# Chunk attention with keys over four heads and norming on GpSimd; modulated attention's shift turned in front of the scores

## The reference, cut to what matters

```python
mod = jax.nn.sigmoid(hidden_states @ cg_W + cg_b + (cons_vec @ am_W + am_b))
scores = scores * mod.transpose(0, 2, 1)[..., None]
probs = jax.nn.softmax(scores, axis=-1)
ctx = jnp.einsum('bhqk,bhkd->bhqd', probs, v)
```

## Time and profile before

| | |
|---|---|
| median of 3 runs | 3992.09 us (3989.94 to 3993.36) |
| profiled execution | 3997.91 us, span 3996.2 us |
| PE, PEld busy | 3580.1 us (90%), 1710.4 us (43%) |
| DVE, ACT, POOL busy | 2339.2 us (59%), 1502.5 us (38%), 1540.2 us (39%) |
| modulated attention | about 212 to 957 us |
| chunk attention | about 2757 to 3020 us |

### The profile page before, as it was taken

The page is one execution under the profiler, slowest core; times in us unless marked ns, Lnnn a source line. Parts: engine busy times, 40 slices in busy tenths (PEclk is TensorE's granted clock), DMA queues, the critical chain, the costliest instruction groups (busy, mean ns, idle before and its releaser), DMA issues. The chain is left out here.

```text
span 3996.2 us, 55438 instructions
## 1 busy us (share of the span) xinstructions
PE 3580.1 (90%) x19176; PEld 1710.4 (43%) x19176; DVE 2339.2 (59%) x3916; ACT 1502.5 (38%) x2216; POOL 1540.2 (39%) x1343
## 2 busy tenths in 40 slices
PE   9989999997999889998789656687998989999995
PEld 4412222222333343333545355443554655655653
DVE  5679999994666326664632458977896631111112
ACT  2237777775444323444222334212553211111112
POOL 0142222222788505887346323144552322222221
PEclk9979999998999999999889766899999989999998
DMA  5622222221112151120622421454442123333333
GB/s 182 209 77 68 76 62 62 69 71 48 36 47 63 58 195 58 43 81 16 187 71 85 150 70 45 164 127 109 131 136 83 34 69 91 103 101 105 100 90 95
DMA packets 309775, 366.44 MB, mean 92 GB/s; under 512 B 54130, under 2 KB 241796, under 8 KB 308548
## 3 DMA queue, kind: packets, MB, share of 16 engines
q1 hardware_dynamic: 269972, 305.81, 24.4%
q0 software_dynamic: 30384, 50.90, 5.5%
q10 hardware_dynamic: 9216, 7.09, 0.6%
HBM read 228.00 MB, written 127.27 MB: 89 GB/s over the span
## 5 line engine op out<-in xcount | busy, mean ns | idle before, releaser
L626 DVE TENSOR_REDUCE modulated_mx<-modulated_ring 128x1 f32<-128x512 f32 x1024 | 651.8, 683 | 43.1 <-PE modulated_ring L533 37.4
L610 ACT ACTIVATE modulated_probs<-modulated_scores 128x1024 f32<-128x1024 f32 x512 | 496.1, 1021 | 189.1 <-PE modulated_scores L554 189.0
L3234 DVE TENSOR_TENSOR expert_h<-expert_gelu,expert_bank 128x512 f32<-128x512 f32 x128 | 88.0, 688 | 390.9 <-PE expert_bank L3163 385.4
L3205 ACT ACTIVATE expert_gelu<-expert_bank 128x512 f32<-128x512 f32 x128 | 76.4, 597 | 549.4 <-PE expert_bank L3163 546.5
L3123 POOL DMA_INDIRECT scratch_acc<-expert_y,expert_idx x64 | 100.8, 1575 | 427.5 <-DVE expert_y L3239 404.2
L1019 POOL TENSOR_TENSOR causal_total<-causal_total,causal_probs 128x1024 f32<-128x1024 f32 x96 | 227.1, 2366 | 59.1 <-ACT causal_probs L928 51.7
L1019 POOL TENSOR_TENSOR meta_total<-meta_total,meta_probs 128x1024 f32<-128x1024 f32 x96 | 227.1, 2366 | 58.7 <-ACT meta_probs L928 51.3
L950 DVE TENSOR_REDUCE meta_mx<-meta_maxima 128x2 f32<-128x1024 f32 x120 | 146.9, 1224 | 117.7 <-PE meta_maxima L815 117.1
L950 DVE TENSOR_REDUCE causal_mx<-causal_maxima 128x2 f32<-128x1024 f32 x120 | 146.9, 1224 | 117.7 <-PE causal_maxima L815 117.1
L928 ACT ACTIVATE meta_probs<-meta_scores 128x1024 f32<-128x1024 f32 x128 | 131.0, 1024 | 142.2 <-PE meta_scores L841 139.3
L928 ACT ACTIVATE causal_probs<-causal_scores 128x1024 f32<-128x1024 f32 x128 | 131.0, 1024 | 142.1 <-PE causal_scores L841 139.1
(11 more groups left out here) (546 smaller groups left out, 7521.2 us busy)
## 6 DMA issues: line engine op xcount, KB each, us to landing
scratch_v<-proj_v SPq DMA_DIRECT2D x8, 1024.0 KB, 6.8
ahead_ctx<-scratch_ctx SPq DMA_DIRECT2D x16, 512.0 KB, 4.7
scratch_M<-steps_snap SPq DMA_DIRECT2D x16, 512.0 KB, 3.3
chunk_raw_v<-scratch_v SPq DMA_DIRECT2D x64, 128.0 KB, 2.8
chunk_mem<-scratch_M SPq DMA_DIRECT2D x32, 256.0 KB, 3.0
first_wg<-x_WgT SPq DMA_DIRECT2D x8, 1024.0 KB, 5.0
first_wu<-x_WuT SPq DMA_DIRECT2D x8, 1024.0 KB, 7.1
first_wd<-x_WdT SPq DMA_DIRECT2D x8, 1024.0 KB, 6.8
```

The source lines that it names most:

```text
L610: nc.scalar.activation(probs[u % NPROBS][i][:], sc[i][:], ACT.Exp, scale=SCALE).then_inc(s_exp, 1)
L626: V.tensor_reduce(mx[h % 2][:, x // 2, 1 - j % 2, j // 2, x % 2:x % 2 + 1], ring[bank_of["max", 4 * m + j]][:], AX.X, ALU.max).then_inc(s_ ...
```

## The change

Modulated attention: PE turns the shift in front of the unit's score products and not behind; ACT copies it in front of the unit's exponentials; and DVE makes it not in one piece behind the last reduction of a half, but in three pieces behind the first, second and fourth reduction of the next unit.

Chunk attention:
- A key is written for four heads and not eight: `own` (128x4) is 1 where a feature belongs to the head with this number among its four. GpSimd needs two multiplications of 512 columns for a tile, not four. The scores take eight products of 64 rows by 64 outputs and 256 columns; the 64 rows of a product hold four heads, and the two halves of the rows write different banks. The heads lie in another order in the scores, and line 2617 of the new code reads them so.
- The norming of the probabilities (`pnorm`) goes from DVE to GpSimd, behind the expansion of the keys of the next tile.
- ACT's exponential of t stands in front of the copy of t-1. PE turns t-1 at the end of slot t, behind the context of t-2.
- In the context, the four memory products stand together and the sixteen value products behind them; the start flag is set on the first alone.
- DVE makes `own` at the stage's start from `blocks`, and GpSimd waits for it.

```diff
--- modulated attention, PE
-                for i in range(2):
-                    scores(u, i)
                 if u in turns:
                     turn_shift(turns[u])
+                for i in range(2):
+                    scores(u, i)
--- modulated attention, ACT
+                if u in turns:
+                    copy_shift(turns[u])
                 for i in range(2):
...
-                if u in turns:
-                    copy_shift(turns[u])
--- modulated attention, DVE
-                    reduce(m)
-                    if m % KT == KT - 1:
-                        make_shift(m // KT)
+                    before = m // KT - 1
+                    made_here = m % KT == 0 and before > 0
+                    reduce(m, range(0, 1))
+                    if made_here:
+                        lowest(before)
+                    reduce(m, range(1, 2))
+                    if made_here:
+                        shift_high(before)
+                    reduce(m, range(2, Q))
+                    if made_here:
+                        shift_rest(before)
--- chunk attention, GpSimd
-                        for c in range(2):
-                            for h in range(HH):
-                                ins = G.tensor_tensor(kexp[j % 2][:, c, h], kT[j][:, h, c * C64:(c + 1) * C64].unsqueeze(1).broadcast_to([P, HP, C64]),
-                                                      blocks[:].unsqueeze(2).broadcast_to([P, HP, C64]), ALU.mult)
+                        for h in range(HH):
+                            ins = G.tensor_tensor(kexp[j % 2][:, h], kT[j][:, h, :].rearrange("p (c k) -> p c k", c=2).unsqueeze(2).broadcast_to([P, 2, QUAD, C64]),
+                                                  own[:].unsqueeze(1).unsqueeze(3).broadcast_to([P, 2, QUAD, C64]), ALU.mult)
                         pool_k.done(ins)
+                    if live(at, j, 1):
+                        o = (j - 1) % 2
+                        dve_rec.wait(pool, t - 1)
+                        pe_turn.wait(pool, t - 3)
+                        pool_normed.done(G.tensor_tensor(normed[o][:], probs[o][:], rec[o][:].unsqueeze(2).broadcast_to([P, H16, C64]), ALU.mult))
--- chunk attention, PE
                         for h in range(HH):
                             for c in range(2):
-                                last = nc.tensor.matmul(sc[c * C64:(c + 1) * C64, h * HP:(h + 1) * HP, :].rearrange("p h k -> p (h k)"),
-                                                        qT[j][:, h, c * C64:(c + 1) * C64], kexp[j % 2][:, c, h].rearrange("p h k -> p (h k)"),
-                                                        start=False, stop=True, skip_group_check=True)
+                                for r in range(ROWS):
+                                    at_rows = slice(r * C64, (r + 1) * C64)
+                                    last = nc.tensor.matmul(sc[c * C64:(c + 1) * C64, r * HP + h * QUAD:r * HP + (h + 1) * QUAD, :].rearrange("p a k -> p (a k)"),
+                                                            qT[j][at_rows, h, c * C64:(c + 1) * C64], kexp[j % 2][at_rows, h, c].rearrange("p a k -> p (a k)"),
+                                                            start=False, stop=True, skip_group_check=True)
...
+                        both = [(c, h, slice(c * C64, (c + 1) * C64)) for c in range(2) for h in range(HH)]
+                        for c, h, toks in both:
+                            nc.tensor.matmul(ctxps[:, h, toks], mem[m][:, c, h * P:(h + 1) * P], qT[m][:, h, toks],
+                                             start=(c + h == 0), stop=False, skip_group_check=True)
+                        for c, h, toks in both:
+                            for r in range(PAIRS // HH):
+                                last = nc.tensor.matmul(ctxps[32 * r:32 * r + 32, h, toks], val[m][:, c, h * (PAIRS // HH) + r, :],
+                                                        probsT[m % 2][:, r // 2 * QUAD + h * 2 + r % 2, toks], start=False, stop=True, skip_group_check=True)
--- chunk attention, DVE
+            V.tensor_reduce(own[:], blocks[:].rearrange("p (a b) -> p b a", b=QUAD), AX.X, ALU.add).then_inc(s_own, 1)
...
+                        pool_normed.wait(dve, t - 3)
                         dve_rec.done(V.reciprocal(rec[o][:], sums[o][:]))
-                        dve_rec.wait(dve, t - 1)
-                        pe_turn.wait(dve, t - 3)
-                        dve_normed.done(V.tensor_tensor(normed[o][:], probs[o][:], heads(rec[o]), ALU.mult))
```

More of the change, by code:

```diff
@@ L2604, in body @@
                         pe_new.done(last)
+                    if live(at, j, 1):
+                        pool_normed.wait(pe, t - 1)
+                        act_probsT.wait(pe, t - 2)
+                        for r in range(PAIRS):
+                            last = nc.tensor.transpose(turned[:, r, :], normed[(j - 1) % 2][:, 2 * r:2 * r + 2, :].rearrange("p a k -> p (a k)"), ident[:])
+                        pe_turn.done(last)
             iterations(pe, body)
```

67 lines of the change are left out of this document (32 added, 35 removed).

## The result

The changed kernel took 3922.6 us (median of 4 runs, 3920.5 to 3923.7) against 3991.0 us (4 runs, 3983.4 to 3993.4): a ratio of 0.9829 with a 95% interval of 0.9817 to 0.9841, or 63 to 73 us less. The forecast was 3947 us in 3930 to 3972. The direction and the mechanism (rival A) came; 45 us were forecast and 68 came, so the time lies 7 us outside the range. The profiled execution took 3921.6 us (span 3919.9).

The account below looks back on a forecast made before the run. PE, busy 90% of 3996.2 us, was priced inside two stages, with a GpSimd loop setting the new chunk iteration. Modulated 18 plus chunk 27 gave 45 us: 3953 profiled, 3947 us as median, range 3930 to 3972.

Parts of the forecast that it names:

- rival A: Whole kernel: both parts gain as summed, 18 + 27 = 45 us, time 3928 to 3966 us; chance 0.66.
- Modulated, DVE's part: Modulated attention: shift operations spread between reductions cost 0.15 us a half of today's 0.41 (bounds 0 and 0.41).
- Modulated, PE and ACT: Modulated attention: turn and copy in front cost 0.5 us a half where 0.84 stood (bounds 0.22 and 1.1).
- The new wait for the bank: Modulated attention: PE, turning before the scores, waits for DVE to free a ring bank, 0.2 to 0.3 us.
- Rival B: Modulated attention gives nothing, the new bank wait taking the place of the copy's; 3965 us, chance 0.12.
- Chunk, PE: Chunk attention: scores 1.05 us (gain 0.8), context 0.45 us off, so PE's slot falls from 6.86 to 5.6 us.
- Chunk, the loop: Chunk attention: dependences through GpSimd over two tiles, 11.5 + 14.1 = 25.6 us; 25.5 taken against 28.88, gaining 27 us.
- the two events of the slow clock: Chunk attention: two stretches at 1.2 GHz behind longer PE idle lengthen the average iteration; left as they are, no gain.
- today's meeting of expansion and multiplication: Chunk attention: GpSimd's expansion and DVE's multiplication exclude each other, expansion 2.03 us instead of 1.04; change removes this.
- C: Chunk attention: GpSimd's operations meet DVE's and hold the loop, iteration 28.5 us; 3971 us, chance 0.14.
- D: Chunk attention: gaps in each slot leave PE at 1.2 GHz for much of the stage, slower, 4024 us; chance 0.08.

Follow-up runs that it names:

- Experiment 8: Changed kernel with the shift turned behind the scores and copied behind the exponentials, as before, still made in three pieces: 3939.2 us, ratio 0.9869.
- experiment 1: Kernel before with the modulated part of the change alone: 3966.6 us, ratio 0.9941.
- Experiment 9: Changed kernel with GpSimd's norming of tile t-2, not t-1, behind the expansion of tile t: 3913.7 us, ratio 0.9810.
- experiment 2: Kernel before with the chunk part of the change alone: 3945.6 us, ratio 0.9890.
- experiment 7: Changed kernel with the shift made in one piece behind a half's last reduction, turn and copy still in front: 3942.9 us, ratio 0.9876.
- experiment 3: Changed kernel with the norming of the probabilities back on DVE: 3956.7 us, ratio 0.9918.
- experiment 6: Changed kernel with the old order: probabilities turned before the context product and copied before the next exponential: 3964.2 us, ratio 0.9928.
- experiment 12: Kernel before with keys over four heads alone (two expansions, eight score products), norming on DVE: 3991.2 us, ratio 0.9997.
- experiment 4: Changed kernel with keys over eight heads again (four expansions, four score products a tile), norming on GpSimd: 3977.3 us, ratio 0.9969.
- experiment 11: Changed kernel with keys a tile ahead (GpSimd norms t-2) and small transposes behind the turning of the probabilities: 3917.8 us, ratio 0.9820.

## Why the prediction was right in kind and short in size

**Modulated, DVE's part.** 0.15 us a half for three operations between reductions; measured 0. Experiment 8 has the pieces alone at 0.41 us a half, all of it.

**Modulated, PE and ACT.** The new wait for the bank was forecast at 0.2 to 0.3 us and is 0.19; turn and wait leave 0.47, the copy 0.01, against 0.5 together. A half costs 0.48 us over eight regular units (20.88) in place of 0.65, so it saves 0.77 in place of 0.60. Over 31 halves that is 24 us, and experiment 1 measured 23.3, for a forecast of 18. Rival B (the new wait takes the place of the copy's) is refuted.

**Chunk, PE.** Scores: 1.03 us, forecast 1.05, so quarters of the array run beside each other. Context: 0.83 saved, forecast 0.45, mis-sized. Slot 5.19 us for 5.6. Neither sets the iteration.

**Chunk, the loop.** Two pairs of tiles, one with the norm, take 11.0 + 13.3 = 24.3 us against 11.5 + 14.1 = 25.6. Term by term: norming 1.90 for 2.2; reciprocal and hand-overs 0.78 for 1 (the loop's 11.0 less 10.22 of the other operations); the norm adds 2.3 for 2.6; the rest within 0.1. Against the 25.5 taken, the 1.2 us are about 10 us over eight iterations. Experiment 9 shows that the loop is the bound, by opening it, and also that it bound by 1.1 us only: in the pair with the norm the last wait is DVE's own queue, which the forecast had as a plain sum of 23.2 and which experiment 9 reached with 23.15. Two sums of the forecast are off by themselves and change little: its terms of the first loop add to 11.6, not 11.5, and PE's idle of an iteration is 25.5 - 4 x 5.6 = 3.1 us, not 2.5.

**The step that failed: "so I leave the two events of the slow clock as they are".** The seven measured iterations are 210.1 us before and 169.9 after. Of these 40.2 us, 7 x (28.88 - 24.26) = 32.3 are the regular iteration, and 5.6 + 4.0 = 9.6 the two long ones of before; the rest, -1.7, is in the short and first ones of both. Each of the two events cost 1.0 us by the longer wait and 4.6 and 3.0 us by the clock behind it. The prediction had the cause in hand, where it says that the change "removes today's meeting of expansion and multiplication", and gave this no term in the sum. That meeting is what made PE wait 2.21 us and not 1.21 in front of both events, and with the norming on GpSimd it is gone; no run removes the meeting by itself. By experiment 1, where both meetings recur and only one slow stretch, 6.6 us of the 9.6 come with the kernel and 3.0 are of one execution. Whether the clock falls behind such a wait, no run lets one foretell.

The slow clock itself is not gone. In the stretch 2802.30 to 2812.00 of after it is 0.82, about 3.5 us at 1.2 GHz, where before has about 10 (0.57 over 12.00 us) and about 7 (0.66 over 10.00). That iteration is 24.71 us, 0.45 over the regular one. The traces of experiments 8, 2 and 7, with the same chunk stage, have one such short stretch each (granted clock 0.93 over the third iteration, as over this one of after) and iterations of 24.60, 25.09 and 26.06 us: 0.34, 0.83 and 1.80 over. So a slow stretch can nearly vanish behind the loop, as PE's 5.19 us of work in 6.06 a tile would let it, but in one of four traces it was paid at about the price of before, 0.5 us for each us at 1.2 GHz. Most of what was saved comes from the waits that are gone and from the shorter stretch, not from PE's slack.

**The other miss, of size only,** is the loop's: norming, hand-overs and norm as above, about 10 us, no less than the events.

Added up: 45 us forecast; about 10 for the loop, 5 to 7 for modulated attention (23.3 to 24.8 by experiment 1's median and trace, for 18) and 6 to 10 for the events make 66 to 72, and 68 was measured.

**The rivals.** C (GpSimd meets DVE and holds an iteration at 28.5) is refuted by mean durations of 1.04 and 1.90 us and by iterations of 24.3 us. D did not happen, though it was near: the granted clock falls to 0.88 or 0.89 over iterations of experiments 3, 6 and 12, each of which lacks a part of the change or more.

**What was wrong in the reasoning behind the parts.** I priced each part by itself and added. The experiments give 34 us for the transfer, 55 for the keys, 42 for the order and 8 for the context: 139 us for a stage that gains 44. And the keys alone gain 0. Each part relieves one engine or the loop. Without the transfer, the keys or the order the iteration stays at 28 to 30 us (experiments 3, 4 and 6); only the context's grouping is a small term, 25.0 us without it.

## What to carry to other kernels

Find the loop of dependences through all engines, not only the busiest engine, and sum it operation by operation; a part that shortens one engine pays only once every other engine and the loop are below the new length. When a slow-clock event or another loss is seen in the profile of before, ask what sets it off and whether the change removes that: here a meeting of two engines did, and its removal was worth 6 to 10 us that no sum held. Treat a wait of PE of 1.5 us or more, inside a busy loop of this kind, as a risk and not as a fixed cost: the same wait was followed by 1.2 GHz in one iteration and not in the next.

## What was not expected of the hardware

- Quarters of the array work beside each other in f32: eight products of 64 rows by 64 outputs and 256 columns take 1.03 us, four of 128 rows by 64 and 512 columns 1.87.
- One and the same wait of PE can be followed by products at 1.2 GHz or not: 1.62 us (experiment 11) and 2.22 us (experiment 12) every second time, 2.21 us twice in before and once of twice in experiment 1, 1.54 us in after at 2807.96 but not at 2857.42. Those of 1.21 in the earlier trace rows were not. No run isolates what else decides.
- A shorter PE slot can give nothing: experiment 12 alternates between 27.5 and 31.0 us an iteration, where before has 28.88.
- A norming on DVE of 1.23 us takes 2.05 to 2.12 beside an expansion on GpSimd (before and experiment 1), as the expansion of the earlier trace rows is held by DVE.
- GpSimd multiplies 128x1024 by a broadcast factor in 1.90 us, where the addition of two full operands in the earlier trace rows takes 2.37.
- Code that no edit touched varied from 1799.6 to 1807.0 us between profiles, so a stage must be read from its own ends, not from the difference of two spans.
